# Eight loads of the next unit's stack issued at slots 2 to 6 in place of 2 to 11 in self-attention units

## The reference

```python
x = x + _L0_attn_ref(_layernorm(x), W_qkv, b_qkv, W_out, b_out)
    # qkv = x @ W_qkv.T + b; 16 heads of 16; q, k rotated by cos/sin
    # softmax(q k^T / sqrt(16)) v, then @ W_out.T + b_out
x = x + _L0_xattn_ref(_layernorm(x), ctx_512, ...)
    # causal softmax attention of x on itself + softmax attention on ctx, then @ Wp + bp
x = x + _L0_ffn_ref(_layernorm(x), Wg, w1, w2)
    # argmax expert of softmax(x @ Wg), capacity 256: relu(x w1) w2, times the gate
```

## Time and profile before

| | |
|---|---|
| median of 3 runs | 1630.7 us (1630.34 to 1641.71) |
| span of the profiled execution, first to last instruction | 1626.3 us |
| TensorE busy | 1443.6 us, 89% of the span |
| DVE, ACT, POOL busy | 1204.3, 1062.0, 650.5 us |
| HBM read and written | 102.33 and 51.18 MB |

### The profile page before, as it was taken

One profiled execution on the slowest core, in us unless ns is written; L12 is line 12 of the kernel. 1 busy time (PEld: TensorE's weight loads), 2 busy tenths in 40 slices (PEclk: granted clock), 3 DMA queues, 4 the chain that ended last, 5 costly groups with the idle time before them and its releaser, 6 DMA issues.

```text
span 1626.3 us, 37857 instructions
## 1 busy us (share of the span) xinstructions
PE 1443.6 (89%) x14610; PEld 647.8 (40%) x14610; DVE 1204.3 (74%) x2434; ACT 1062.0 (65%) x2139; POOL 650.5 (40%) x535
## 2 busy tenths in 40 slices
PE   3799999999999898898998989989989978779997
PEld 1222322333333433334334244333343432359997
DVE  6788878888876776776877877768778677537774
ACT  2377777778777676676676676766766656425662
POOL 2544565466422422236145333352352211225554
PEclk8699999999999999999999999999999999889999
DMA  6435344444323433323323322332333211157771
GB/s 179 115 119 141 105 112 115 120 115 112 92 60 95 110 88 101 90 83 104 82 83 88 104 80 69 96 98 71 85 100 97 60 45 39 48 189 262 251 259 62
DMA packets 119479, 175.82 MB, mean 108 GB/s; under 512 B 26273, under 2 KB 85895, under 8 KB 114696
## 3 DMA queue, kind: packets, MB, share of 16 engines
q1 hardware_dynamic: 111376, 158.50, 34.4%
q0 software_dynamic: 5888, 14.24, 2.7%
q10 hardware_dynamic: 2048, 0.83, 0.2%
HBM read 102.33 MB, written 51.18 MB: 94 GB/s over the span
## 4 chain that ended last, share of the span: by engine, by line
PE 54%; DVE 17%; DMA 9%; ACT 6%; issue 6%; POOL 5%; SPq 2%; POOLq 0%; DVEq 0%; ACTq 0%
PE psO L741 13%; PE psM L466 9%; PE psS L764 9%; DVE negmax L1193 9%; PE psK L466 6%; PE psK L795 6%; PE psS L466 4%; ACT probs L1029 4%; DMA recipB<-recip_scratch 3%; PE psK L693 2%; DVE xn L1165 2%; DMA shared<-shared 1%; DVE stats L1141 1%; DMA stack<-mrows 1%; PE psM L831 1%
## 5 line engine op out<-in xcount | busy, mean ns | idle before, releaser
L1193 DVE TENSOR_REDUCE negmax<-psS 128x1 f32<-128x512 f32 (+3 forms) x1536 | 869.4, 615 | 273.6 <-PE psS L764 136.4
L1029 ACT ACTIVATE probs<-psK 128x512 f32<-128x512 f32 (+3 forms) x1536 | 753.7, 544 | 325.3 <-PE psK L795 198.4
L741 PE MATMUL psO<-probs,V 128*32 128x256 f32 (+1 forms) x5632 | 446.1, 389 | 23.8 <-ACT U L1021 17.8
L764 PE MATMUL psS<-stack 48*128 48x512 f16 (+3 forms) x1536 | 284.5, 367 | 57.2 <-DVE negmax L1193 53.7
L795 PE MATMUL psK<-stack 50*128 50x512 f16 (+3 forms) x1536 | 278.5, 359 | 26.1 <-DMA stack<-mrows 14.7
L764 PEld LDWEIGHTS psS<-stack 48*128 48x128 f16 x1536 | 74.2, 93 | 373.2 <-DVE negmax L1193 290.7
L741 PEld LDWEIGHTS psO<-probs,V 128*32 128x32 f32 x5632 | 113.5, 109 | 210.9 <-issue 122.8
L1427 POOL TENSOR_TENSOR rstd<-lnt,minus_half 128x4 f32<-128x4 f32 x24 | 24.7, 1028 | 193.1 <-DVE lnt L1157 193.1
L795 PEld LDWEIGHTS psK<-stack 50*128 50x128 f16 x1536 | 76.5, 95 | 57.4 <-ACT probs L1029 23.6
L1553 POOL DMA_INDIRECT out_dram<-stack,put_to x32 | 76.8, 2399 | 17.8 <-issue 9.1
L1441 POOL CAST shared<-shared 128x512 f16<-128x512 f32 x8 | 4.9, 612 | 191.2 <-ACT shared L1051 191.2
(11 more groups left out here) (192 smaller groups left out, 2063.1 us busy)
## 6 DMA issues: line engine op xcount, KB each, us to landing
spare<-in_L_ffn_w_dram SPq DMA_DIRECT2D x32, 1024.0 KB, 6.3
parts_scratch<-parts SPq DMA_DIRECT2D x192, 128.0 KB
stack<-parts_scratch SPq DMA_DIRECT2D x96, 256.0 KB, 4.0
stack<-parts_scratch SPq DMA_DIRECT2D x96, 128.0 KB, 4.2
packed<-U SPq DMA_DIRECT2D x192, 64.0 KB
recipB<-recip_scratch SPq DMA_DIRECT2D x48, 256.0 KB
shared<-shared SPq DMA_DIRECT2D x48, 128.0 KB, 2.1
probs<-back_scratch POOLq DMA_DIRECT2D x16, 258.0 KB, 3.1
```

The source lines that it names most:

```text
L741: mm = nc.tensor.matmul(psO[32 * i:32 * i + 32, q0:q1], v_of(par)[:, kt, 2 * g + i % 2 + PAIRS * (i // 2), :], probs[:, (unit + i % 2) % P ...
L764: mm = nc.tensor.matmul(psS[:, banks[hh], 0:n], stack_of(par, 0)[rows, hp, qt * P:(qt + 1) * P], stack_of(par, 1)[rows, hp, 0:n], start=Tr ...
L1029: nc.scalar.activation(probs[:, t % P_RING, i, q0:T], psK[:, S_BANKS[t][i], q0:T], ACT.Exp, scale=SM_SCALE / (1 if b.kind == "A" else WSCA ...
L1193: nc.vector.tensor_reduce(negmax[:, g % 2, at:at + 1], psS[:, S_BANKS[u // 2][j], 0:n], AX_X, ALU.max, negate=True).then_inc(s["max_done"], 1)
```

## The change

The table of form "AA" gives the loads other slots. Loads 0 and 1 stay at slots 2 and 3. Loads 2 to 7 stood at slots 6, 7, 8, 9, 10 and 11; now they stand at 4, 4, 5, 5, 6 and 6.

```diff
     "AA": {"v0": (1, 2), "v1": (3, 4), "xT0": (7,), "xT1": (8,), "proj0": (12,), "proj1": (15,), "proj2": (18, 20),
-           "proj3": (22, 23), "out0": (25,), "out1": (26, 27), "ln": (1, 3, 4, 6), "load": (2, 3, 6, 7, 8, 9, 10, 11),
+           "proj3": (22, 23), "out0": (25,), "out1": (26, 27), "ln": (1, 3, 4, 6), "load": (2, 3, 4, 4, 5, 5, 6, 6),
            "split": (8, 8), "lower": (19, 22, 26, 30), "store": (22, 23, 30, 31), "recip": 7, "norm": 13, "attn": 15, "bias": 1},
```

## The result

The changed kernel takes 1620.2 us in the median of 20 runs, against 1631.18 us for 20 runs of the kernel before. The ratio is 0.9941, 95% interval 0.9918 to 0.9964, that is 9.6 us less (6 to 13). The ratio leaves out the runs over 1.5% above the fastest of their kernel, so it is not the quotient of the two medians. The forecast was 11.0 us less, 1619.7 us, with a range of 1615 to 1630. Single runs of one kernel lie up to 30 us apart, so in what follows the profile is read by the stopwatch of the prediction wherever a few us matter: the distance between two L867, eight slots apart. What such a distance takes beyond an undisturbed unit is called the loss.

What follows compares the result with a forecast made beforehand. TensorE was taken to lose 12.4 us to `mrows` waits and the low clock behind them. Of this 12.0 won, less 1.0 lost at slot 8, makes 11.0 us: 1630.7 to 1619.7 us, range 1615 to 1630.

Steps and rivals of the forecast that it cites:

- The loss that can be taken back, 12.4 us: Slots 13 to 29, units 1 to 5: TensorE's time beyond undisturbed stretches, 12.4 us, of which 12.0 was to be won.
- The cause, a burst behind the inverse's reads that holds the swap and the pair of slot 13: Loads 3 to 7, 1 MB behind the inverse's reads, delay small transfers and cause `mrows` waits at slots 16 and 24.
- Slot 8, 1.0 us lost: L795 of slot 8 waits 0.2 us a unit for the `mrows` pair behind loads 2 and 3; five units, 1.0 us.
- a wait of 0.2 us or more at slot 8 is certain in all five units: Remark from a queue-order rule: the slot 5 pair can't count as landed ahead of load 3, so the wait is certain.
- The bound of 8 us: Upper bound of the loss at slot 8 over five units, from waits of 0 to 1.6 us each.
- The inverse, 0.5 us earlier: Slots 5 to 13: store lands later, but reads have the queue alone, take 5.5 us and land half a microsecond earlier.
- the two rates that were given as bounds: Landing of the loads ahead of the inverse's store: 1.2 us or 2.0 us for 256 KB.
- the lead: POOL's L1502 comes earlier by 0.8 to 3.2 us a unit, to cover the waits at slot 24.
- the rival "the inverse comes late": Reads land 3.4 us later, POOL's lead goes, waits at slot 24 stay or grow; about 1629 us, chance 0.18.
- The swap, the pair of slot 13, the waits for `mrows` at slots 16 and 24, the clock: Swap of slot 12 and pair find an empty queue; waits go but for 0.4 us, and the low clock too.
- The signs named beforehand: Profile checks: `mrows` waits under 2 us, only at slot 8; L867 12.96 and 13.9 us apart; L1473 not past 14.6.

Runs made afterwards that it cites:

- e7: Changed kernel with loads 6 and 7 moved from slot 6 to slot 13; ratio 0.9895 to the kernel before.
- e4: Changed kernel with loads 4 to 7 moved to slots 13, 13, 14, 14; ratio 0.9894 to the kernel before.
- e5: Changed kernel with loads 4 to 7 put back at slots 8, 9, 10, 11; ratio 0.9981 to the kernel before.
- e1: Changed kernel with load 2 back at slot 6 and loads 3 to 7 at 13, 13, 13, 14, 14; ratio 0.9952 to the kernel before.
- e2: Changed kernel with loads 2 to 7 all at slot 4, ahead of the `mrows` pair of slot 5; ratio 1.0085 to the kernel before.

## Why the prediction was right, and where its sum was off

The total came within 1.4 us of the forecast and inside the interval of the ratio. By the stopwatch the change brings 8.2 us where the sum has 11.0: two terms were mis-sized, in opposite directions, slot 8 by 0.7 us and the inverse by 3.5.

*The loss that can be taken back, 12.4 us.* Right: e7 takes back all of it and e4 all but 0.2. The stopwatch against unit 5 and unit 1 gave it to 0.1 us; the 8.6 us of waiting alone would have been too little.

*The cause, a burst behind the inverse's reads that holds the swap and the pair of slot 13.* Right, by e4, e5 and e7, and by e1, which shows that earliness is not the point.

*Slot 8, 1.0 us lost.* Too much: slots 5 to 13 lose 0.4 us where they lost 0.1, and the 0.3 more stand in unit 2 alone. That a wait of 0.2 us or more at slot 8 is certain in all five units, as the prediction says beside this term, did not come true, and did not follow from its own bounds, which begin at a wait of 0. Load 3 itself landed in time in four units, 3.9 to 4.5 us behind the L867 of slot 5, and only in unit 2, 5.0 us behind it, was it late; whether the pair passed it cannot be seen where nobody waits. The bound of 8 us was not idle: e2 shows the same wait with more ahead of it.

*The inverse, 0.5 us earlier.* This is the step that failed in size. Times in us of the changed kernel:

| unit | store issued to reads issued | reads issued to L1473 | L1473 behind the L867 of slot 5 | loss in slots 13 to 21 |
|---|---|---|---|---|
| forecast | 3.4 | 5.5 | 14.0 | 0 |
| 1 | 4.2 | 6.4 | 15.8 | 1.4 |
| 2 | 3.9 | 4.9 | 13.9 | 0.0 |
| 3 | 3.8 | 5.3 | 14.2 | 0.0 |
| 4 | 4.2 | 5.2 | 14.5 | 0.3 |
| 5 | 5.0 | 6.2 | 16.4 | 2.1 |

The store lands with the loads ahead of it, as the prediction says, but the loads take 1.3 to 1.8 us for 256 KB from load 3 to load 7, not 1.2, between the two rates that were given as bounds. In units 1 and 5 the reads are slower too, against the 5.5 us that the prediction took from an undisturbed row. In unit 1 they do not have the queue alone, since the load of `X` follows them, which may be the reason but is not tested; why they take 6.2 us in unit 5 stays open. The step behind it failed with it: POOL's L1502 was followed, where the lead held (it starts 17.6 to 18.2 us behind slot 5 in units 2 to 4, against 17.7 forecast), but not ACT's cast, which needs L1473 as well and stands ahead of the exponentials. So the late inverse costs 3.9 us at slot 16 in units 1, 4 and 5, by a road that the rival "the inverse comes late" did not name: it put the price on slot 24.

*The swap, the pair of slot 13, the waits for `mrows` at slots 16 and 24, the clock.* All as forecast: the L1502 of slot 13 waits for no swap in any of the five units, slots 21 to 29 take 13.87 us, PEclk stays at 1.00 in the three units read above.

*The signs named beforehand.* What remained was to be waits for `mrows` at slot 8; it is waits for ACT at slot 16. L867 was to stand 12.96 us apart from slot 13 to 21 in all units; it does in units 2 and 3. The prediction called itself wrong if L1473 starts later than 14.6 us behind slot 5; in units 1 and 5 it starts 15.8 and 16.4 behind. So by its own sign the step on the inverse was wrong, though the total lay in the range.

Whole runs scatter by more than the forecast was off, so the agreement of the total within 1.4 us is partly luck; what the experiments confirm is the 12.4 us, the two places, and the 3.9 us that stayed.

## What to carry to other kernels

Large transfers that nobody waits for still have a price: that of every small transfer issued behind them on the way to an engine that does wait. Look for the stretches of the queue with no small urgent transfer behind them, and put the large ones there, in pieces that have landed before the next urgent one is issued; here four, or six, loads early and the rest behind slot 13 lose less by the stopwatch (0.3 to 1.7 us) than all early (4.3) or five of eight late (6.2); the intervals of the ratios overlap in part. When a value comes later, follow every engine that reads it, in order of its list, not only the one that was the bottleneck before.

## What was not expected of the hardware

A 32 KB store behind 512 KB, 768 KB and 1.25 MB of loads took 2.3, 4.2 and 5.9 us in the median, against 1.5 alone. It looks as if the third 256 KB cost more than the first two together, but the landings in unit 3 of the changed kernel say otherwise. The times to landing of loads 3, 4, 5 and 7, issued at 249.4, 252.15, 252.5 and 253.5:

```profile
DMA to landing us min/median/max: 4.5/4.5/4.5
DMA to landing us min/median/max: 3.1/3.1/3.1
DMA to landing us min/median/max: 4.1/4.1/4.1
DMA to landing us min/median/max: 4.6/4.6/4.6
```

So they land at 253.9, 255.3, 256.6 and 258.1, and each 256 KB takes 1.3 to 1.5 us. The store is issued at 254.43, when a part of the 768 KB has landed, and the reads that wait for it follow load 7 at 258.27. In units 1 to 4 the store lands about 0.2 us behind load 7, in unit 5 1.1.

A fixed program scatters much more than it looks from few runs: 35 runs of the kernel before lie between 1613.3 and 1654.96 us, while the distances of L867 in undisturbed stretches agree to 0.02 us from kernel to kernel.
